# Two matched layouts: W_e in slices of 32 neighbouring rows, and x turned and sorted to fit, with new orders in the head

## The reference

```python
# x (128, 128, 512), cond (128, 512), weight_matrix (1024, 512), W_proj (512, 512), b_proj (512)
u = gelu(cond @ W_proj + b_proj)                    # exact gelu
W_u, W_e = weight_matrix[:512], weight_matrix[512:]
out = x + (u @ W_u)[:, None, :] + einsum('bnd,dc->bnc', x, W_e)
```

## Time and profile before

| | |
|---|---|
| time, median of 3 runs | 344.43 us (344.35 to 344.52) |
| the profiled execution | 344.49 us, its span 342.2 us |
| PE busy | 337.0 us, 98% |
| POOL busy | 285.0 us, 83% |
| DVE busy | 263.2 us, 77% |
| ACT busy | 249.1 us, 73% |
| chain that ended last | PE 97%, DMA 2% |
| memory traffic | 206 GB/s over the span |

### The profile page before, as it was taken

One profiled execution on the slowest core, in us unless ns is written; L12 is line 12 of the kernel. 1 busy time (PEld: TensorE's weight loads), 2 busy tenths in 40 slices (PEclk: granted clock), 3 DMA queues, 4 the chain that ended last, 5 costly groups with the idle time before them and its releaser, 6 DMA issues.

```text
span 342.2 us, 7873 instructions
## 1 busy us (share of the span) xinstructions
PE 337.0 (98%) x2700; PEld 328.6 (96%) x2700; DVE 263.2 (77%) x301; ACT 249.1 (73%) x429; POOL 285.0 (83%) x206
## 2 busy tenths in 40 slices
PE   7999999999999999999999999999999999999996
PEld 3869999999999999999999999999999999999996
DVE  2999997777887777888777789777778877778811
ACT  4577787778777777877777877777787777788741
POOL 3499999988889898889898888989888888888860
PEclk9999999999999999999999999999999999999999
DMA  7996799978888987888998787898878899787216
GB/s 309 290 201 184 170 231 244 238 197 213 202 187 193 244 221 197 207 204 178 220 230 221 196 211 191 177 245 219 218 186 220 178 205 245 203 209 204 92 49 230
DMA packets 73065, 70.64 MB, mean 206 GB/s; under 512 B 2912, under 2 KB 68448, under 8 KB 68704
## 3 DMA queue, kind: packets, MB, share of 16 engines
q1 hardware_dynamic: 73056, 70.53, 81.4%
HBM read 36.96 MB, written 33.55 MB: 206 GB/s over the span
## 4 chain that ended last, share of the span: by engine, by line
PE 97%; DMA 2%; DVE 0%; SPq 0%; ACT 0%; issue 0%; DVEq 0%
PE banks L877 31%; PE banks L881 30%; PE banks L879 30%; PE banks L796 2%; DMA w_e<-in_L_cond_weight_matrix 2%; PE banks L845 2%; PE banks L863 1%; PE banks L781 0%; PE banks L835 0%; PE banks L838 0%; PE banks L841 0%; DVE w_hi L715 0%; SPq L268 0%; ACT y L612 0%; DVEq L714 0%
## 5 line engine op out<-in xcount | busy, mean ns | idle before, releaser
L877 PE MATMUL banks<-t_hi,hi 128*128 128x256 f32 x496 | 140.6, 283 | 0.1
L881 PE MATMUL banks<-t_hi,lo 128*128 128x256 f32 x496 | 140.4, 283 | 0.0
L879 PE MATMUL banks<-t_lo,hi 128*128 128x256 f32 x496 | 140.4, 283 | 0.0
L877 PE MATMUL banks<-w_hi,hi 128*128 128x256 f32 x372 | 105.4, 283 | 0.0
L879 PE MATMUL banks<-w_lo,hi 128*128 128x256 f32 x372 | 105.3, 283 | 0.0
L881 PE MATMUL banks<-w_hi,lo 128*128 128x256 f32 x372 | 105.3, 283 | 0.0
L617 DVE STREAM_TRANSPOSE work<-quad_raw 128x1024 f32<-128x1024 f32 (+1 forms) x62 | 100.4, 1619 | 0.0
L877 PEld LDWEIGHTS banks<-t_hi,hi 128*128 128x128 f32 x496 | 95.2, 192 | 0.4 <-issue 0.2
L881 PEld LDWEIGHTS banks<-t_hi,lo 128*128 128x128 f32 x496 | 95.2, 192 | 0.0
L879 PEld LDWEIGHTS banks<-t_lo,hi 128*128 128x128 f32 x496 | 95.2, 192 | 0.0
L366 POOL TENSOR_TENSOR lo<-work,hi 128x1024 fp32r<-128x1024 f32 x31 | 74.9, 2417 | 17.4 <-ACT hi L469 17.4
(11 more groups left out here) (83 smaller groups left out, 410.4 us busy)
## 6 DMA issues: line engine op xcount, KB each, us to landing
out<-y SPq DMA_DIRECT2D x31, 1024.0 KB, 4.5
quad_raw<-in_x SPq DMA_DIRECT2D x120, 256.0 KB, 5.8
w_e<-in_L_cond_weight_matrix SPq DMA_DIRECT2D x1, 1024.0 KB, 5.6
w_proj_sb<-in_L_cond_W_proj SPq DMA_DIRECT2D x1, 1024.0 KB, 8.0
w_u<-in_L_cond_weight_matrix SPq DMA_DIRECT2D x1, 1024.0 KB, 9.1
quad_raw<-in_x SPq DMA_DIRECT2D x8, 128.0 KB, 8.1
out<-y SPq DMA_DIRECT2D x3, 256.0 KB, 2.1
head_raw<-in_x SPq DMA_DIRECT2D x1, 512.0 KB, 3.5
```

The source lines that it names most:

```text
L877: pe.matmul(psum[:, t, :], a_hi[:, 2 * j + t, :], b_hi[:, j, :], start=False, stop=False, skip_group_check=True)
L879: pe.matmul(psum[:, t, :], a_hi[:, 2 * j + t, :], b_lo[:, j, :], start=False, stop=False, skip_group_check=True)
L881: last = pe.matmul(psum[:, t, :], a_lo[:, 2 * j + t, :], b_hi[:, j, :], start=False, stop=(j == T - 1), skip_group_check=True)
```

## The change

1. **W_e.** Partition 32q + k of slice j now holds row 128q + 32j + k: four groups of 32 neighbouring rows for each slice. Each slice is loaded by a transfer of its own, with 2 KB for each partition, and has a semaphore of its own. The place of the identity and its pattern on POOL follow.
2. **x to match.** DVE's turns read neighbouring elements in place of every fourth. Two tiles no longer merge into one access pattern, so each turn of two tiles becomes two instructions, one for each tile.
3. **Direct tiles sorted.** The columns that a flip must take no longer lie at one fixed step. DVE copies direct tile 0 and ACT direct tile 1 into the new order (L255) before PE flips them.
4. **New orders in the head.** Two more warm-up matmuls before the flips and four fewer behind them. ACT: cond_hi between the second and the third proj_hi; h before t_hi(0); t_hi(2) and t_hi(3) behind up(0). DVE: cond_lo behind the second proj_lo, turn_second(0) between the third and the fourth. POOL: t_sum(0) waits for three proj_lo only; t_lo(1) and t_lo(2) move behind up_lo(0), the low part of a22 of quad 0 to the end. PE: in h the products with cond_lo come ahead of those with proj_lo.

```diff
 QUAD = 4
-WARM_UP = 7
-WARM_ON = 5
+WARM_UP = 9
+WARM_ON = 1
...
     w_u_dram = weight_matrix[0:D, :].rearrange("(p j) c -> p j c", j=NJ)
-    w_e_dram = weight_matrix[D:2 * D, :].rearrange("(p j) c -> p j c", j=NJ)
+    w_e_dram = weight_matrix[D:2 * D, :].rearrange("(q j k) c -> q k j c", q=NQ, j=NJ)
     w_proj_dram = w_proj.rearrange("(p j) c -> p j c", j=NJ)
...
         second = head_raw[:, T * TILE:HEAD * TILE].rearrange("p (m n w) -> p m n w", m=NM, n=T)
+        sorted_rows = [rows[:, :].rearrange("p (j q k) -> p j q k", j=NJ, q=NQ) for rows in snap_rows[2:4]]
         direct_psum = [banks[2][:, t, :].rearrange("p (j b) -> p j b", j=NJ) for t in range(T)]
...
         b_proj_loaded = sem("b_proj_loaded")
-        w_e_loaded = sem("w_e_loaded")
+        w_e_loaded = [sem(f"w_e_loaded{j}") for j in range(NJ)]
         direct_loaded = sem("direct_loaded")
         second_loaded = sem("second_loaded")
+        direct_sorted = [sem(f"direct_sorted{t}") for t in range(T)]
         direct_flipped = sem("direct_flipped")
...
+        def sort_direct(engine_copy, t):
+            return engine_copy(sorted_rows[t], direct[:, t, :].rearrange("p (q j k) -> p j q k", q=NQ, j=NJ)).then_inc(
+                direct_sorted[t], 1)
         def diagonal(j):
-            return w_e[:, j, :].rearrange("p (a r) -> p a r", r=NJ)[:, :, j]
+            return w_e[:, j, :].rearrange("p (q r k) -> p r q k", q=NQ, r=NJ)[:, j]
...
             sp.dma_start(direct, x[:, 0:T, :]).then_inc(direct_loaded, 16)
-            sp.dma_start(w_e[:, :, :], w_e_dram).then_inc(w_e_loaded, 16)
+            for j in range(NJ):
+                sp.dma_start(w_e[:, j, :], w_e_dram[:, :, j, :]).then_inc(w_e_loaded[j], 16)
             sp.dma_start(cond_sb[:, :], cond).then_inc(cond_loaded, 16)
...
             pool.wait_ge(first_eye_zeroed, 1)
-            pool.affine_select(out=first_eye, in_=first_eye, compare_op=ALU.not_equal, fill=1.0,
-                               base=0, pattern=[[-1, C]], channel_multiplier=NJ).then_inc(first_eye_ready, 1)
+            eye_view = first_eye.rearrange("p (q j k) -> p q j k", q=NQ, j=NJ)
+            pool.affine_select(out=eye_view, in_=eye_view, compare_op=ALU.not_equal, fill=1.0, base=0,
+                               pattern=[[-Q, NQ], [4 * P, NJ], [-1, Q]], channel_multiplier=1).then_inc(first_eye_ready, 1)
...
                 diag = diagonal(j)
-                pool.tensor_tensor(diag, diag, ident[:, :], ALU.add).then_inc(done, 1)
-            pool.wait_ge(w_e_loaded, 16)
+                pool.tensor_tensor(diag, diag, ident[:, :].rearrange("p (q k) -> p q k", q=NQ),
+                                   ALU.add).then_inc(done, 1)
+            pool.wait_ge(w_e_loaded[1], 16)
             add_ident(1, w_diag_ready)
-            add_ident(2, w_diag_ready)
             pool.wait_ge(w_hi_ready[0], 1)
             add_ident(0, first_diag_ready)
-            add_ident(3, w_diag_ready)
+            for j in range(2, NJ):
+                pool.wait_ge(w_e_loaded[j], 16)
+                add_ident(j, w_diag_ready)
...
             b11, b12, b21, b22 = b_of[:, 0, 0], b_of[:, 0, 1], b_of[:, 1, 0], b_of[:, 1, 1]
-            pool.wait_ge(proj_lo_ready, NJ)
             pool.wait_ge(w_diag_ready, NJ - 1)
             pool.wait_ge(first_diag_ready, 1)
+            pool.wait_ge(proj_lo_ready, NJ - 1)
             pool.tensor_tensor(t_sum[:, 0, :, :], b12, b11, ALU.subtract).then_inc(t_summed, 1)
+            pool.wait_ge(proj_lo_ready, NJ)
             pool.tensor_tensor(t_sum[:, 2, :, :], b22, b12, ALU.subtract).then_inc(t_summed, 1)
...
                                    ALU.subtract).then_inc(up_lo, 1)
+                if first:
+                    split_t(1)
+                    split_t(2)
                 if second:
...
                 if first:
-                    split_a22()
                     split_s2()
...
                     split_s4()
+                    split_a22()
                 else:
...
-            for n in range(3):
-                split_t(n)
+            split_t(0)
             prepare(0, 0, True)
...
             act.copy(eye_psum, first_eye).then_inc(first_eye_copied, 1)
+            act.wait_ge(direct_loaded, 16)
+            sort_direct(act.copy, 1)
             for n in range(T):
...
                 act.copy(w_hi[:, j, :], w_e[:, j, :]).then_inc(w_hi_ready[j], 1)
+            def hi_proj(j):
+                act.copy(proj_hi[:, j, :], w_proj_sb[:, j, :]).then_inc(proj_hi_ready, 1)
             act.wait_ge(w_proj_loaded, 16)
-            for j in range(NJ):
-                act.copy(proj_hi[:, j, :], w_proj_sb[:, j, :]).then_inc(proj_hi_ready, 1)
+            hi_proj(0)
+            hi_proj(1)
             act.wait_ge(cond_flipped, 1)
             act.copy(cond_hi, flip_psum).then_inc(cond_hi_ready, 1)
+            hi_proj(2)
+            hi_proj(3)
...
             direct_hi(T)
-            hi_t(0)
             act.wait_ge(h_summed, 1)
             act.copy(h[:, :], h_psum).then_inc(h_ready, 1)
+            hi_t(0)
             act.wait_ge(h_flipped, 1)
...
             hi_t(1)
-            hi_t(2)
-            hi_t(3)
...
             up(0, 0, True)
+            hi_t(2)
+            hi_t(3)
             seed_a(0, 0, True)
...
-            by_block = "p (j r) (i m) -> p m j (r i)"
+            def turn(slots, rows):
+                for r in range(T):
+                    last = transpose(slots.rearrange("p (j r) (i m) -> p r m j i", r=T, m=NM)[:, r], rows[:, r])
+                return last
...
                     rows = raw_rows(quad_raw[p], QUAD)[:, :, n * T:(n + 1) * T, :]
-                return rows.rearrange("p m n (k j) -> p m j (n k)", k=Q)
+                return rows.rearrange("p m n (j k) -> p n m j k", k=Q)
...
                     dve.wait_ge(s4_ready, k - 1)
-                transpose(a_up[p].rearrange(by_block, r=T, m=NM), raw_tiles(p, 0, first)).then_inc(up_turned, 1)
+                turn(a_up[p], raw_tiles(p, 0, first)).then_inc(up_turned, 1)
...
                     dve.wait_ge(s3_ready, k)
-                transpose(a21.rearrange(by_block, r=T, m=NM), low[:, :, 0:2, :]).then_inc(a21_turned, 1)
+                turn(a21, low[:, :, :, 0:2]).then_inc(a21_turned, 1)
                 if not first:
                     dve.wait_ge(a22_lo, k - 1)
-                transpose(a22[p].rearrange(by_block, r=T, m=NM), low[:, :, 2:4, :]).then_inc(a22_turned, 1)
+                turn(a22[p], low[:, :, :, 2:4]).then_inc(a22_turned, 1)
...
                 transpose(direct_psum[t].rearrange("p j (i m) -> p m j i", m=NM),
-                          second[:, :, t, :].rearrange("p m (k j) -> p m j k", k=Q)).then_inc(second_turned, 1)
+                          second[:, :, t, :].rearrange("p m (j k) -> p m j k", k=Q)).then_inc(second_turned, 1)
...
+            dve.wait_ge(direct_loaded, 16)
+            sort_direct(dve.tensor_copy, 0)
             dve.wait_ge(first_eye_copied, 1)
-            dve.wait_ge(w_e_loaded, 16)
+            dve.wait_ge(w_e_loaded[0], 16)
             dve.tensor_tensor(w_hi[:, 0, :], w_e[:, 0, :], eye_psum, ALU.add).then_inc(w_hi_ready[0], 1)
...
                 split_w(j)
-            for j in range(NJ):
+            def split_proj(j):
                 dve.wait_ge(proj_hi_ready, j + 1)
...
                                   ALU.subtract).then_inc(proj_lo_ready, 1)
+            split_proj(0)
+            split_proj(1)
             dve.wait_ge(cond_hi_ready, 1)
             dve.tensor_tensor(cond_lo, flip_psum, cond_hi.bitcast(F32), ALU.subtract).then_inc(cond_lo_ready, 1)
+            split_proj(2)
             dve.wait_ge(second_loaded, LOADS)
...
             turn_second(0)
+            split_proj(3)
             split_direct(T)
...
             for t in range(T):
-                pe.wait_ge(direct_loaded, 16)
-                flip(direct_psum[t], by_j(direct[:, t, :]), direct_flipped)
+                pe.wait_ge(direct_sorted[t], 1)
+                flip(direct_psum[t], snap_rows[T + t][:, :].rearrange("b (j p) -> b j p", j=NJ), direct_flipped)
             warm(WARM_ON)
...
                 pe.matmul(h_psum, cond_hi[:, j, :], proj_hi[:, j, :], start=(j == 0), stop=False)
+            pe.wait_ge(cond_lo_ready, 1)
+            for j in range(NJ):
+                pe.matmul(h_psum, cond_lo[:, j, :], proj_hi[:, j, :], start=False, stop=False)
             for j in range(NJ):
                 pe.wait_ge(proj_lo_ready, j + 1)
-                pe.matmul(h_psum, cond_hi[:, j, :], proj_lo[:, j, :], start=False, stop=False)
-            pe.wait_ge(cond_lo_ready, 1)
-            for j in range(NJ):
-                last = pe.matmul(h_psum, cond_lo[:, j, :], proj_hi[:, j, :], start=False, stop=(j == NJ - 1))
+                last = pe.matmul(h_psum, cond_hi[:, j, :], proj_lo[:, j, :], start=False, stop=(j == NJ - 1))
             last.then_inc(h_summed, 1)
```

## The result

| | us | ratio to before (95%) |
|---|---|---|
| before, 4 runs beside it | 344.47 (344.35 to 344.52) | |
| after, 4 runs | 358.15 (358.11 to 358.40) | 1.0397 (1.0384 to 1.041) |
| predicted | 344.2 (343.6 to 345.1) | |

The profiled execution took 358.40 for a span of 356.1 (before: 344.49 and 342.2). The change costs 13.7 us.

What follows compares the result with a forecast made beforehand. PE was taken as the bound, with POOL's chain up to up_lo(1) deciding its wait in the head. Of 1.1 gained in PE's head 0.3 survives: 344.49 less 0.3 is 344.2, range 343.6 to 345.1.

Steps and rivals of the forecast that it cites:

- The sorting: Head, before PE's flips: DVE sorts direct tile 0 in 0.43, ACT tile 1 in 0.62, both done by 4.9.
- the cuts of the turns: DVE's turns split per tile: 0.11 for one cut, 0.3 for three in a quad; PE's stream hides it in the middle.
- Four slices of 262 KB then land 0.63 apart: 4.9, 5.5, 6.2, 6.8.: Head, load of w_e: slices at about 415 GB/s, so PE's first product starts at 6.4 instead of 7.62.
- slices "at 300 GB/s": Part of the slower rival, 15% together: later loads and POOL 0.9 later, time 345.1.
- Loads wait in the queue, not for SP: Head, DMA queue: three more issues push later ones back by 2.2 us at most, covered by some 5 us of queued bytes.
- I cost this at nothing: Head: the later issues on SP were priced at zero; quad 0's fourth load still lands at 17.65.
- The conflict: Head: proj_lo(3) on DVE beside POOL's t_sum(0), both reading SBUF; taken at 0.05, bounds nothing and 0.4.
- The rows of w_lo: Earlier trace, DVE: w_lo(0) overlapped POOL's end and took 0.73 against 0.68 for the others; source of the 0.05.
- the gap of 0.44: POOL's wait ahead of up_lo(0), from 20.5 to 20.9, for ACT's up(0) behind the load landing at 17.65.
- POOL's start: Head: t_sum(0) waits for the third proj_lo and begins at 13.75, against 13.71 before; nothing won.
- The turns: DVE's turns of 512 elements: taken at 1.11, bounds 0.68 and 2.1; at 0.68 the gain is 0.6.
- Rival 2: DVE's turns are faster with neighbouring elements: gain 0.6, time 343.9; chance 13%.

Runs made afterwards that it cites:

- block slices: Kernel after, but slice j of w_e is one block of 128 neighbouring lines of W_e (output not the reference's); 345.11, ratio 1.0021.
- whole load: Kernel after, but w_e comes by the one old transfer with 8 KB lines, everything else of the change kept; 345.75, ratio 1.0038.
- orders only: Kernel before with only the new orders of the head, w_e in one transfer, old layout, no sorting; 345.76, ratio 1.004.
- whole load with old orders: Kernel after with w_e by the one old transfer and the old orders; sorting, turns and warm-ups of the change stay; 344.18, ratio 0.9992.

## Why the prediction was wrong

**Right.** What bounds the kernel: PE dense behind the head, POOL's chain ahead of m1(1). The sorting at 0.43 and 0.62, done by 4.9. The middle. That the cuts of the turns cost nothing there: DVE is busy for 60.26 of 80 where the earlier trace rows has 63.60.

**The step that failed** is "Four slices of 262 KB then land 0.63 apart: 4.9, 5.5, 6.2, 6.8." I carried over the 415 GB/s of w_e and the 428 of the earlier trace rows because the lines of cond have the same length. The window of the earlier trace rows didn't even show those lines: w_e itself, with its 8 KB lines, lands at 6.78 and fills most of it. What decided was another thing: cond's source has 128 lines as its slowest dimension, the slice's has 4, and that sets how many engines move it. 102 GB/s follow and, with the rest of the loads behind them, 13.0 us. The rival with slices "at 300 GB/s" had the right side and place, not the size: it took a known rate for slightly uncertain, while the pattern itself was new. The far bound was missing: no row of before had a transfer with so small a slowest dimension, so nothing bounded it from below.

**"Loads wait in the queue, not for SP"** held for before and was carried over; with slow slices SP is held for 2.50 and 4.24 at one issue, and quad 0's load lands at 32.0 instead of 17.65. Its cover, 5 us of queued bytes, was gone. "I cost this at nothing" is the second step that failed, and it is the one that the chain of waits runs through. It fails on a small scale with good slices too: at block slices the same load is issued at 9.88 instead of 9.45 and lands at 18.44.

```profile
9.88 8.56 DMA quad_raw<-in_x
18.47 2.08 DVE work L642 x2
20.57 1.05 ACT hi L492
21.70 2.38 POOL lo L382
```

**The conflict.** I took 0.05, with 0.4 as the upper bound. proj_lo(3) takes 1.47 at block slices and at whole load, 1.30 after, 1.10 with orders only, and 0.68 alone. At block slices it starts at 14.64 and ends at 16.11; t_sum(0) runs from 14.26 to 15.55, and 0.56 are left behind it, nearly a whole proj_lo; in all nine traces in which the two run side by side it is 0.55 or 0.56, wherever proj_lo(3) starts. So the later instruction waits out the other one. The rows of w_lo, which seemed to speak against it, had met only the last moments of POOL, and fit: w_lo(0) ends 0.54 behind POOL (8.69 + 0.73 against 8.35 + 0.53). The Trainium skill (SBUF — State Buffer, Who interferes with whom) has that rule; these traces agree. In the sum the conflict gives the 0.63 of waiting ahead of t_sum(2), where I had 0.36. My upper bound was also added up wrong: 0.4 fits into the gap of 0.44, and no 0.1 is left over.

**POOL's start.** With slices as assumed t_sum(0) starts at 14.26, not 13.75, since PE's first product comes at 6.59 instead of 6.4 and the flips of cond at 11.51 instead of 11.1. Together with the conflict POOL is free for up_lo(0) at 21.33, where I had 20.5 and a gap up to 20.9. It then waits 0.37 more, to 21.70, for the late load of quad 0. So of the 0.8 by which up_lo(0) is late, POOL's own chain accounts for 0.4 and the load for the rest. Up_lo(1) is ready at 35.24 instead of 34.53, and m1(1) starts at 35.29 instead of 34.61. That is the 0.7 between 344.2 and the profiled 344.87; the median, 345.11, lies 0.2 above it, within the scatter. A gain of the new orders isn't seen here.

**The turns.** The row for 512 elements, 1.11, was taken for both targets. Turns into PSUM (`banks`) are faster at stride one, 0.72 for 512 elements; those into SBUF (`work`) are not:

```profile
L642 DVE STREAM_TRANSPOSE work<-quad_raw 128x512 f32<-128x512 f32 x62 | 64.7, 1125 | 3.7 <-DMA quad_raw<-in_x 3.7
L642 DVE STREAM_TRANSPOSE work<-quad_raw 128x256 f32<-128x256 f32 x62 | 33.9, 625 | 0.0
L642 DVE STREAM_TRANSPOSE banks<-quad_raw 128x256 f32<-128x256 f32 x62 | 24.9, 447 | 0.1
L642 DVE STREAM_TRANSPOSE banks<-head_raw 128x512 f32<-128x512 f32 x2 | 1.4, 718 | 0.1
```

From 256 to 512 elements a turn into PSUM takes 271 ns more, 1.06 ns for each element, and one into SBUF 500 ns, 1.95 for each. The full rate of the Trainium skill (Vector Engine (DVE) Microarchitecture Reference, 3.8 The reshape front-end and per-opcode configuration), which I had weighed as a lower bound, is reached with the one and not with the other (1125 ns for 512, as before). Rival 2 was half right and worth nothing that can be told (whole load with old orders, 344.18).

No version here beats the kernel before by more than a measurement tells. By these runs the layout would need a transfer that reaches all 128 partitions with a slowest dimension that 16 divides; none was found that keeps its order of rows.

## What to carry to other kernels

Before carrying over the rate of a transfer, compare its pattern from the outside in: the slowest dimension of source and target, the partitions it covers, the step between its lines; equal lines say little. Then ask what stands behind it in the queue: a slow transfer makes every later one late, and here it was one of those, quad 0's load, that held the end. An order that fills one engine's gap is worth what the next engine in the chain leaves of it: read when each operand is ready, not when it is asked for.
